# A four-block conv and scan model on one core: a written order for every engine, step vectors with stationary weights, and no products of constants

## The reference

```python
x = x + L0(gn(x))   # 1x1, 3x3, 1x1 convolution; weights mixed per sample from 8 experts (routing by channel means)
x = x + L1(gn(x))   # selective scan, see below
x = x + L2(gn(x))   # 1x1 convolution, offsets, deformable 3x3 convolution, 1x1 convolution
x = x + L3(gn(x))   # 1x1, 3x3, 1x1, each squared: (y + 1)**2, then a batch norm
```

```python
xf  = silu(depthwise_conv3(x_ssm) + dw_b)
dbc = einsum('oc,bcn->bon', dbc_w, xf) + dbc_b        # 34 rows: 2 heads x (1 + 8 + 8)
dt  = softplus(dbc[:, :, 0]);  B_t, C_t = dbc[:, :, 1:9], dbc[:, :, 9:]
x_h, dt, B_t, C_t = gather(x_h), gather(dt), gather(B_t), gather(C_t)      # by perm
y   = scan(...);  y = gather(y, inverse perm);  y = y * silu(gate) + res
x   = silu(out_proj_w @ y + out_proj_b)
```

## Time and profile before

| | us |
|---|---|
| three runs | 1046.47, 1044.54, 1045.98 (median 1045.98) |
| the profiled execution, its own time | 1048.19 |
| its span, first to last instruction | 1046.0 |
| PE busy | 935.8 (89%), weight loads beside it 635.9 |
| DVE busy | 731.9 (70%) |
| ACT busy | 550.1 (53%) |
| POOL busy | 362.4 (35%) |
| mean granted TensorE clock | 0.971 of full speed |

### The profile page before, as it was taken

The page is one execution under the profiler, slowest core; times in us unless marked ns, Lnnn a source line. Parts: engine busy times, 40 slices in busy tenths (PEclk is TensorE's granted clock), DMA queues, the critical chain, the costliest instruction groups (busy, mean ns, idle before and its releaser), DMA issues.

```text
span 1046.0 us, 19785 instructions
## 1 busy us (share of the span) xinstructions
PE 935.8 (89%) x7460; PEld 635.9 (61%) x7460; DVE 731.9 (70%) x2047; ACT 550.1 (53%) x1155; POOL 362.4 (35%) x320
## 2 busy tenths in 40 slices
PE   3788988999999899999999999999999998887766
PEld 2555656666666566666666666666666665646454
DVE  2567377786878587878878687878787868756332
ACT  1143353756556474748475655657474747361412
POOL 3013433435251625344342525152524343342200
PEclk9889999999999999999999999999999999889998
DMA  9101153352626253544536262626353444426060
GB/s 220 37 8 44 40 141 121 85 177 75 184 75 178 70 169 108 145 128 116 161 94 188 76 190 72 182 79 168 96 164 113 128 130 118 147 64 189 15 207 16
DMA packets 116547, 123.33 MB, mean 118 GB/s; under 512 B 64802, under 2 KB 99750, under 8 KB 116454
## 3 DMA queue, kind: packets, MB, share of 16 engines
q1 hardware_dynamic: 107812, 105.45, 34.6%
q0 software_dynamic: 6144, 13.71, 4.6%
q10 hardware_dynamic: 2498, 2.91, 1.2%
HBM read 84.31 MB, written 37.73 MB: 117 GB/s over the span
## 4 chain that ended last, share of the span: by engine, by line
PE 30%; DVE 24%; issue 17%; POOL 13%; ACT 9%; DMA 5%; SPq 1%; ACTq 0%; POOLq 0%; DVEq 0%
PE ps L625 27%; DVE c_w L1301 4%; ACT y L986 3%; POOL rs L1215 3%; POOL b_ex L1215 3%; POOL b_cr L1215 2%; POOL b_yp L1263 2%; ACT L986 2%; POOL b_res L1215 2%; DVE y L1306 2%; DVE x L1309 2%; DVE st L1336 2%; DMA b_yp<-y_turned,b_to 2%; DVE b_xf L1309 1%; DVE y L1309 1%
## 5 line engine op out<-in xcount | busy, mean ns | idle before, releaser
L1263 POOL DMA_INDIRECT b_yp<-y_turned,b_to x64 | 90.3, 1411 | 271.5 <-DMA y_turned<-b_yt 256.9
L625 PE MATMUL ps<-y,inw 128*128 128x392 f32 x384 | 140.2, 509 | 1.3 <-DVE y L1306 1.3
L1215 POOL TENSOR_TENSOR rs<-ve,root 128x4 f32<-128x4 f32 x64 | 66.1, 1032 | 200.9 <-DVE ve L1305 200.4
L1336 DVE BATCH_NORM_STATS2 st<-x 128x6 f32<-128x196 f32 x256 | 73.7, 350 | 88.0 <-POOL x L1215 76.0
L1301 DVE TENSOR_TENSOR c_w<-c_w,c_hat 126x1176 f32<-126x1176 f32 (+1 forms) x64 | 97.8, 1580 | 11.2 <-DMA c_w<-hat_turned 11.2
L625 PE MATMUL ps<-c_w,c_zt 126*64 126x196 f32 x896 | 88.7, 345 | 11.6 <-DVE c_w L1301 6.9
L625 PEld LDWEIGHTS ps<-y,inw 128*128 128x128 f32 x384 | 70.6, 194 | 46.4 <-issue 6.8
L625 PE MATMUL ps<-w,a_S 128*32 128x384 f32 (+2 forms) x1280 | 81.6, 392 | 7.5 <-DVE a_S L1309 5.7
L625 PE MATMUL ps<-c 128*128 128x256 f32 (+1 forms) x284 | 86.7, 442 | 0.0
L986 ACT ACT_TABLE_LOAD x50 | 64.2, 1283 | 37.5 <-PE ps L625 36.7
L625 PEld LDWEIGHTS ps<-c_w,c_zt 126*64 126x64 f32 x896 | 63.8, 142 | 31.8 <-issue 14.3
(11 more groups left out here) (203 smaller groups left out, 2025.3 us busy)
## 6 DMA issues: line engine op xcount, KB each, us to landing
c_w<-hat_turned SPq DMA_DIRECT2D x32, 771.8 KB
c_w<-hat_turned SPq DMA_DIRECT2D x32, 578.8 KB
z_turned<-c_z SPq DMA_DIRECT2D x32, 441.0 KB
c_zt<-z_turned SPq DMA_DIRECT2D x16, 882.0 KB
b_xp<-x_turned SPq DMA_DIRECT2D x32, 222.0 KB
x<-in_x SPq DMA_DIRECT2D x32, 196.0 KB, 2.7
y_turned<-b_yt SPq DMA_DIRECT2D x32, 196.0 KB
out<-x SPq DMA_DIRECT2D x32, 196.0 KB, 7.3
```

Source lines behind the costliest of these rows:

```text
L625: return nc.tensor.matmul(o, l, r, start=start, stop=stop)
L1215: return nc.gpsimd.tensor_tensor(out=o, in0=x, in1=y, op=op)
L1263: nc.gpsimd.indirect_dma_start(out=YP[:, m, h].rearrange("p b d -> p (b d)"), out_offset=None, in_=y_dram[g % 2], in_offset=bass.IndirectO ...
L1336: last = nc.vector.bn_stats(st[s][:, 2 * c + b, :], x[:, c, b, :])
```

## The change

Four things are changed.

1. **Order.** `PLAN` and `FROM` go. `ORDER` has a string for each engine with one letter for each step: the letter names the stage, and the n-th "s" is the n-th step of s1, counted through its groups. So any order is possible, at the start and at the end too. All five engines get a new one; in its middle the string repeats with each group. SP loads the input of group 1 ahead of the weights.
2. **PSUM banks.** A string `BANKS` says which of the seven banks each tile takes, in place of the turn.
3. **Step vectors.** ta has a part with 4 products of 196 columns, the weights `dbcw` stationary (64 columns wide, of which 34 are real) and `b_xf` moving. ACT adds the bias in its copy to `b_row`, two transposes bring the rows to pixel order, and DVE copies them into `XT` beside the transposed `b_xf`. The eight transposes of `b_xf` go into two tiles of 512 columns (before: four of 290), so ACT and DVE copy one each. DVE's addition of the bias after the load is gone; `xq` is now a view of `b_xp`, and what waited for `b_xq_ok` waits for the load.
4. **Products of constants.** `keep_busy` and its calls are gone, and `BUSY` is empty.

```diff
-    def take(self, f, g):
-        self.turn[f, g] = len(self.turn)
+    def take(self, f, g):
+        bank = int(self.banks[len(self.turn)])
+        self.turn[f, g] = bank, self.uses[bank]
+        self.uses[bank] += 1
...
-BUSY = {("n0", 1): 1, ("r3", 0): 1, ("w3", 0): 1, ("r1", 1): 5, ("n1", 0): 1, ("r1", 2): 6, ("n1", 1): 10, ("n2", 0): 7,
-        ("acc", 14): 12, (("pt", 0), 15): 6, (("pt", 1), 15): 6, ("acc", 15): 20, ("n3", 15): 7, ("d1", 15): 7,
-        ("d2", 15): 4}
+BUSY = {}
+LETTERS = "acbstuofgdhkz"
+ORDER = {
+    "tensor": (
+        "aaccccccccczczccbcczsssssscctttctacccccbacscsssssuuuuuuutttutccuuccccoooouuuuufuuccgcubgcgggsuuggggg"
...
-                lo = at128["expand"][0]
-                for _ in range(n):
-                    mm(t[:, 0:2 * N], ident, c128[:, lo:lo + 2 * N])
...
             def ta(i, part, g):
...
+                if i == 0:
...
+                    for h in range(HEADS):
+                        for b in range(G):
+                            last = nc.tensor.transpose(t[0:HT, (h * G + b) * HD:(h * G + b + 1) * HD],
+                                                       b_xf[:, h, b, tt * HT:(tt + 1) * HT], ident)
+                    last.then_inc(R.filled(("xt", tt), g), 1)
+                if i == 1:
...
+                    t = take("db", g)
+                    for c in range(CC):
+                        for b in range(G):
+                            last = mm(t[half(b), 0:N], dbcw[:, c, :], b_xf[:, c, b, :], start=(c == 0), stop=(c == CC - 1))
+                    last.then_inc(R.filled("db", g), 1)
+                if i == 3:
+                    drained(pe, "db", g)
+                    t = take("rows", g)
+                    for tt in range(2):
+                        last = nc.tensor.transpose(t[0:HT, tt * 128:(tt + 1) * 128], b_row[:, tt * HT:(tt + 1) * HT], ident)
+                    last.then_inc(R.filled("rows", g), 1)
...
             def f2(i, part, g):
-                if i == 0:
-                    keep_busy("c1", g, 1)
...
-                    tt(xq[:, :, :], XP[:, :, :, :, HD:XD].rearrange("p t h b x -> p (t h b) x"), b_bc[:, :, :], ALU.add)\
-                        .then_inc(b_xq_ok.sem, 1)
+                    filled(v, "rows", g)
+                    for tt in range(2):
+                        last = copy(XT[:, tt, :, :, HD:XD], R.tile("rows", g)[0:HT, tt * 128:(tt + 1) * 128]
```

More of the change, by code:

```diff
@@ L327, in planned @@
 def planned(name):
-    todo = []
-    for s, stage in enumerate(STAGES):
-        at = -1
-        for g in range(1 if stage == "once" else GROUPS):
-            for (i, part), start in zip(places(name, stage), PLAN[name][s], strict=True):
-                at = max(start + FROM[stage][g], at + 1)
-                todo.append((at, s, g, i, part))
-    return sorted(todo)
+    todo = {}
+    for letter, stage in zip(LETTERS, STAGES, strict=True):
+        todo[letter] = iter([(stage, g, i, part) for g in range(1 if stage == "once" else GROUPS)
+                             for i, part in places(name, stage)])
+    return [next(todo[letter]) for letter in ORDER[name]]
 def for_groups(name, steps):
-    for _, s, g, i, part in planned(name):
-        steps[STAGES[s]](i, part, g)
+    for stage, g, i, part in planned(name):
+        steps[stage](i, part, g)
 def first(g):
@@ L516, in build, with ring @@
         ps = [ctx.enter_context(nc.psum_tensor(f"ps{i}", [128, 512], F32)) for i in range(8)]
-        def ring(name, which):
+        def ring(name, which, banks):
             return Ring([ps[i] for i in which], ([sem(f"{name}_filled{i}") for i in which],
-                                                 [sem(f"{name}_drained{i}") for i in which]))
-        R = ring("ring", range(7))
-        H = ring("held", [7])
+                                                 [sem(f"{name}_drained{i}") for i in which]), banks)
+        R = ring("ring", range(7), BANKS)
+        H = ring("held", [7], "0" * (GROUPS + 5))
         def sig(name, per=1):
@@ L1234, in ta @@
                 if h == 0:
-                    for b in range(G):
-                        drained(pool, ("xt", 2 * m + b), g)
+                    drained(pool, ("xt", m), g)
+                    if m == 0:
+                        drained(pool, "rows", g)
                 nc.gpsimd.indirect_dma_start(
@@ L1493, in tb @@
                     m = part
+                    if m == 0 and first(g):
+                        v.wait_ge(tables, 1)
                     ins = tt(MD[:, 4 * m:4 * m + 4, :].rearrange("p (h b) c -> p h b c", b=G),
@@ L1828, in once @@
                     sp.wait_ge(ld_w[0], 16 * E4)
-                    for t, name in ((inw, "inw"), (cvec, "cvec"), (dbcw, "dbcw"), (outw, "outw")):
+                    for t, name in ((inw, "inw"), (cvec, "cvec"), (outw, "outw")):
                         load(t[:], a[name], ld_s)
+                    load(dbcw[:, :, 0:HEADS * DBC], a["dbcw"].rearrange("p c h x -> p c (h x)"), ld_s)
                     early = at128["ident"][0]
@@ L1845, in once @@
                         load(d3w[half(b), :], a["d3w"], ld_d)
+                        load(dbcb[b * MID:b * MID + HEADS * DBC, :],
+                             a["rows"][0:1, ROW_DBC:ROW_OFF].rearrange("o k -> k o"), ld_d)
                         load(offb[b * MID:b * MID + 2 * TAPS, :],
```

263 lines of the change are left out of this document (102 added, 161 removed), and 8 rows, old and new, of the table PARTS.

## The result

The changed kernel takes 1131.05 us (median of 4 runs, 1124.50 to 1134.82), the kernel before 1045.26 in the same series (1043.49 to 1046.47): 1.0815 times as long, interval 1.076 to 1.0871. The forecast was 1010 us with 981 to 1043 about it, and 0.82 on faster. It was wrong in size and in sign.

A forecast was written before the change was run, and what follows sets the result against it. PE was taken to bound the middle, one group's way through engines and transfers the ends. Middle -11.4, start -9, end -19.5, lower clock +1.5 sum to -38.4: 1048.19 becomes 1010 us, 80% range 981 to 1043.

The forecast's parts named there:

- 0.5 for a slower clock in some periods: Middle periods: 0.5 us added to each period's walk for a slower clock in some periods.
- the clock falls in every period: Rival: clock falls behind n2 and again later, 1.7 us twice a period, period 57.9, total 1058 us; 14%.
- the wait for the `c_w` product: Middle period: place where the slower-clock rival put the second fall; PE expected to wait 1.5 us ahead of d2.
- The total of 1058: Whole kernel under the slower-clock rival: twelve periods 695, start 184, end 105 and 72, outside 2.2 us; 14%.
- The one fall that I had measured, at 350: Profile before, around 346 to 356: clock fell to 0.50 with PE little busy; 1.7 us of clock missing.
- 0.4 us for it in the walk: Middle period, gather of y: 0.4 us in the walk, and another 0.4 for late gathers.
- The walk of a period: Middle period from n2's sums: 35.9 until the deformable sum plus 18.5 gives 54.4; with 0.9 added, 55.3 against 56.25 us.
- The three waits that I saw ahead of it: PE ahead of the deformable sum: waits of 1.5 us there, about 0.5 at s1 and 0.5 at the scan's output.
- Behind it I had 18.5: From the deformable sum to the next n2, PE is the bound: 18.1 us of work and 0.4 for y's gather.
- The waits behind n2: PE idle 1.6 + 0.5 us at y's halves, 0.7 ahead of `a_md,r1x`, 1.1 ahead of the offsets: 3.9 us.
- The ends: Start 180 for 188.8 us, 9 less; groups 13 to 15 97 for 116.5, 19.5 less; lower clock 1.5 more.
- the signs set down for "wrong": Clock of 0.5 in every period; PE waits on DMA of `b_yp` over 1 us each period; last stretch beyond 72 us.

The follow-up runs named there:

- e6: Kernel before, with its order, banks and products of constants, plus the changed kernel's step vectors: 1045.24 us, ratio 1.000.
- e7: Kernel before with the new step vectors and without any product of constants: 1098.26 us, ratio 1.051.
- e5: Changed kernel with both stores of y_turned moved ahead of the last of the four c_w loads on SyncE: 1094.96 us, ratio 1.050.
- e8: e5 plus three products of constants ahead of y,c1w and one ahead of c_pad,offw: 1087.50 us, ratio 1.042.
- e1: Changed kernel with products of constants back, one ahead of y,c1w and two ahead of c_pad,offw in every group: 1120.90 us, ratio 1.072.
- e9: Kernel before, products kept, with the last c_w load moved ahead of the two stores of y_turned: 1096.77 us, ratio 1.049.
- e3: Kernel before, with its order and banks, without any product of constants: 1092.83 us, ratio 1.044.
- e12: e8 with the stores of y_turned ahead of the last two c_w loads, not one: 1164.16 us, ratio 1.109.

## Why the prediction was wrong

**The sum of the causes.** One way from the old kernel to the new: step vectors 0 (e6), products away +53 (e7 less e6), new order with the load's place as before -3 (e5 less e7, intervals overlap), the load ahead of `y_turned` +36 (changed kernel less e5). Together +86. The sum closes by its making, since each term is a difference of neighbours on the way; the way matters. In the new order, products at the `y` wait give back 7 us (e5 to e8), not 53. One reason is that a late `b_yp` lets the clock fall again in some periods (e8). The other is DVE, which has hardly a pause behind n2. With the fall behind `y` the deformable sum starts 38.7 us after n2's sums (changed kernel, e5), with products and no fall 37.4 (e1, e8), and DVE is done with its part at 36.7 in e8. So the fall behind `y` can cost no more than some 2 us there, and the products give back 1.3 (worked out from these rows; the new order without both was not run).

**The slow clock, the step that failed.** This is the step of the prediction that failed first: I priced it at 0.5 us a period ("0.5 for a slower clock in some periods") and gave the rival "the clock falls in every period" 14%, since the twelve periods before had kept 1.00. They had kept it because of the products that the change takes away: the evidence came from under the cover whose removal was the question. The rival named the first place and not the second: it looked for the second fall at the wait for the `c_w` product, where PE didn't stand, and it came behind `b_yp`. Its price was low too: two falls of 1.7 us are 3.4, and the period shown lacks 8% of its clock, 4.9 us of 61.04. The total of 1058 was 73 us short. The one fall that I had measured, at 350, was already of the second kind; PE's row there shows that it waited for the gather of y.

```profile
350.49 0.53 PE L859 MATMUL ps<-c,b_yp 98*128 98x98 f32 x4 [1.91 <-DMA b_yp<-y_turned,b_to]
```

The period around it took 59.92 us where its neighbours took 55.9: wait and fall together cost 4 us. At the full clock, with four products of constants in it, a period of the new order takes 56.5 to 57.6 us (e8); with neither fault mended it takes 61.5. Without the products the new order was never seen at the full clock.

**The gather of y, the second.** I had 0.4 us for it in the walk and 0.4 more beside it. SyncE's order was before me, and I did not ask which loads `y_turned` stands behind, nor how many bytes of them were still to be moved. It was 1.9 us of waits in the period shown and the second fall of the clock; the part that hangs on the one load's place is 36 us (e5).

**The walk of a period.** Without both faults I had 54.4; e8 has 56.47 at best. It was DVE that I let begin the deformable sum at 35.9; in e8 DVE does go with hardly a pause to the second `c_w` product, as foreseen, but ends it at 36.7 for 35.5, and the sum begins at 37.4 and waits for nobody, for PE, its products of constants with it, goes without a pause from 443.98 to 470.82. The three waits that I saw ahead of it (1.5, 0.5 and 0.5 us) are not there, since PE itself comes later. Behind it I had 18.5, measured 19.07. In e8 PE bounds the period, as in the kernel before. The waits behind n2 came as forecast: 2.02 and 0.24 us at the halves of `y` (1.6 and 0.5 foreseen), 0.75 at the offsets (1.1).

**The ends.** s1 of group 1 begins at 92.76 (91 foreseen), that of group 15 7 us after n2 of group 13 (7 foreseen): the order was read rightly. What follows took 101.6 us for 89, and 112 for 90. Both ways hold waits for `b_yp` (up to 3.64 us in the start) and run at a low clock, 0.86 in the start (0.94 before) and 0.82 in the third stretch (0.91 before). In the end there is also a wait that I had not seen: ACT stood for 19.19 us at a step of group 15's scan, and `d_h`, which it could have made, was queued behind it.

```profile
996.33 0.21 ACT L934 ACTIVATE b_ab<-b_xp 98x8 f32<-98x8 f32 x1 [19.19 <-DMA b_xp<-x_turned]
996.57 0.51 ACT L934 ACTIVATE d_h<-ps,bias,bn_q 128x196 f32<-128x196 f32 x1
```

```profile
997.14 1.68 PE L571 MATMUL ps<-d_h,d3w 64*128 64x196 f32 x8 [15.66 <-ACT d_h L934]
```

What this wait costs was not tried. Nor was the bank table alone: the new order with its banks in turn was not run, so the table and the order are one cause here. And e8 is 42 us over the kernel before, 37.8 in the two profiled spans: 9.5 in the start, 19.5 in the 11 periods and 8.8 in the rest; which steps of the order make them is open.

**Right:** no product of `c` alone; the step vectors at no cost; DVE with hardly a pause from n2 to the second `c_w` product; PE's pauses behind n2 and their releasers. Two of the signs set down for "wrong" showed (the clock of 0.5 in every period; waits of over 1 us for `b_yp`), and the third, 72 us, was just reached (72.06).

## What to carry to other kernels

Before products of constants are taken out, ask what the clock would be without them; a trace that shows a clock of 1.00 with them in is no evidence. A store that someone waits for paid here for the loads issued ahead of it, and another queue did not change that, so in a new order compare, for every store that someone waits for, what was issued before it; and before a load is moved back, look at what is queued on its reader's engine behind the wait for it. A wait of 2 us on PE costs more than 2 us when the clock falls behind it, and filler that fits the waits of one order must be measured anew in another. And look at every period, not at one: in e1 the clock fell behind `y` in one of 11, in e5 in all.

## What the runs showed of the hardware

Two stores of 196 KB took 4.0 us from their issue to the first gather in the kernel before and 4.4 in e5, each with one `c_w` load of 771.8 KB behind them. With it ahead they took 6.1 us in the old order (e9) and 7.9 in the new one (the changed kernel), though it had been issued 12 or 5 us earlier. Over the 11 periods the medians are 4.0, 4.9, 5.8 and 8.2. ScalarE's queue for the stores alone changed nothing (42.2 and 41.7 us after n2's sums). The clock, once fallen, stayed low through work that kept PE busy: from 692 to about 699 in the changed kernel, from 557.7 to 564 in e3. It fell behind waits of PE of 2.0 us (changed kernel), 1.1 and 1.5 (e3), 2.9 (e9) and 4.65 us (e12), and in e1 it stood at 1.00 behind a wait of 1.07.
